# Edge counts from a column of ones in the gather table, with four changes of order in a graph block on one Trainium2 core

## The chip, the cores and the metric

The kernel runs on one core of one Trainium2 chip. TensorE (PE) multiplies matrices, VectorE (DVE), ScalarE (ACT) and GpSimd (POOL) work on tiles of 128 partitions, and SyncE (SP) issues DMAs. ACT and POOL issue DMAs too. The metric is the device time of one execution in microseconds (us): the median over timed runs.

## The reference, cut to what matters

6250 nodes have rows of 256 numbers, and 100,000 edges lead from `src` to `dst`; `dst` is sorted and skewed, so the first nodes have many more edges than the last.

```python
xn = layernorm(x)
# (1) mean over the incoming edges
Wh  = xn @ W + b
h   = segment_sum(Wh[src], dst) / maximum(segment_sum(ones, dst), 1)
# (2) linear attention over all nodes, 8 heads, feature map elu + 1
x1  = x + h + attention(xn) @ wo + bo
# (3) top-1 mixture of 8 experts, at most 977 rows each
logits = layernorm(x1) @ gate_w + gate_b;  e = argmax(softmax(logits))
y   = (relu(layernorm(x1) @ w1[e] + b1[e]) @ w2[e] + b2[e]) * prob[e]
out = x1 + y
```

## The kernel before, in words

The nodes are 49 tiles of 128 rows. One program per engine is written by hand; semaphores (`S["..."]`, counted up, waited for with `wait_ge`) are all that orders the engines.

**Prologue.** Rows are normalised; each is split into a high fp16 part and a scaled low fp16 part (`tall`, 512 fp16 columns, low part times 2048) and stored in DRAM as `table`. Then the keys of all tiles are projected and summed (`project`, `sum_keys` on PE; `keys`, `features` on DVE and ACT), and the matrix `ms` of the attention is formed. While this goes on, POOL already gathers for tile 0 and PE adds one group of edges in 25 of these key steps (`TICKS`, `sum_some`).

**Gather.** POOL gathers the table rows of 128 edges with one indirect DMA (L566); four such are a group, and `gathered` is a ring of `RQ = 7` groups. There are 196 groups, 784 gathers. A group whose edges fall in two tiles is summed for both, so PE and DVE handle 244 (group, tile) pairs. For each pair DVE builds four one-hot matrices (L1291, ring `onehot` of `OQ = 4`), and PE adds `onehot^T @ gathered` to the PSUM bank `pA` (L875). Before the change, PE also adds `ones^T @ onehot` to the bank `pD` (L878): its diagonals hold the number of edges of each node. `slots` tells POOL that a ring place is free, `oh_slots` the same of a one-hot buffer to DVE.

**Steps.** After `ms`, all engines run `step(t)` for t = 0 to 50. In step t, DVE does in this order: `late` (remaining one-hots), `degrees(t)` (count, L1359 to L1365), `next_tile` (up to four one-hots of tile t+1), `combine(t)`, `node_out(t-1)`, `place(t-2)`, `plan`, `shares(t)`, `queries(t+1)`, `residual(t)` (L1380, L1382), `route(t-1)`, `post` of a job. PE does `project_sum(t-1)` (L940 to L944), `count`, `query` (L921), `divisor` (L929), `expert` (L966), `hidden` (L975), the transposes `turn_sums` (L984) and `turn_rows` (L992), then the edge sum of tile t+1. ACT does `ready` (L680), `query` (L692), `divisor`, `job_rows`, `deviation`, `hidden` (relu, L730), `softmax` (L708), `columns` (L722, copies the transposes and signals `t_sb`, for which PE's next `project_sum` waits). POOL scatters the rows of a tile to their expert (L519) when it is five groups past the end of the tile two later, and writes out a finished job (`finish`, L506); both stand in its queue between gathers.

**Jobs.** A job is 128 rows of one expert. From step `T0 = 10` on each step runs the middle part of one job: `plan(t - T0 + LEAD)` three steps ahead picks the first expert that has 128 unserved rows among the tiles placed so far, and a dummy job (rows of a pad tile, nothing written) if none has. What is left after step 50 (`END`), partly filled tiles included, runs in a tail loop of `expert`, `hidden`, `turn_rows` on PE and `post` and `plan` on DVE.

**Weights.** ACT issues eight DMAs of 1 MB (L673) for all output weights `w2s` right after `ms` and before its `query(0)`. SP loads the first-layer weights `w1b` of each job in two halves (L402).

The wait that ends a job's relu is one semaphore for all eight pieces:

```python
for h, (name, ph) in enumerate((("h0_ps", pH0), ("h1_ps", pH1))):   # ACT hidden, L727
    a.wait_ge(S[name], j + 1)
    for c in range(FC // 2): ins = a.activation(...)                  # L730
ins.then_inc(S["h_sb"], 1)                                            # L732
```

## Time and profile before

| what | value |
|---|---|
| median of 3 timed runs | 1618.29 us (1617.28 to 1618.33) |
| span of the profiled execution | 1943.8 us |
| PE, weight load, DVE, ACT, POOL busy | 65%, 43%, 49%, 26%, 47% |
| granted TensorE clock, mean | 0.823 |
| first gather starts | 92.08 us |
| `ready(0)`, `ready(23)`, `ready(48)` on ACT (L680) | 333.36, 1182.07, 1783.04 us |
| last job's write (L506) | 1934.87 us |

The span runs from the first to the last instruction of the profiled execution; the page shows no other time of that execution, and it lies 325.5 us above the median of the timed ones. Times of rows are us from the start of the span. A step is best read from one L680 to the next, since there is one per tile.

### The profile page before, as it was taken

What the parts mean: (1) busy time and instruction counts of PE and PEld (TensorE: products, weight loads), DVE (VectorE), ACT (ScalarE), POOL (GpSimd) and SP (SyncE); (2) the same over time, 40 slices, a digit from 0 to 9 for tenths busy, and PEclk for the clock granted to TensorE, in tenths of its full rate; (3) what the DMA queues carried; (4) which work ended last, traced back from release to release, by engine and by line L of the source; (5) the groups of instructions that cost most, each with busy time, mean ns of one, the idle gap of its engine ahead of it and who ended that gap; (6) DMA issues with size and microseconds to landing.
All of it is one profiled execution on the core that took longest, in us unless ns stands there. A gap on an engine that the chain in (4) does not pass through costs nothing.

```text
span 1943.8 us, 34137 instructions
## 1 busy us (share of the span) xinstructions
PE 1260.6 (65%) x5864; PEld 828.4 (43%) x5865; DVE 957.9 (49%) x3464; ACT 510.3 (26%) x1337; POOL 917.5 (47%) x963
## 2 busy tenths in 40 slices
PE   3666673355454464767656676786786887887785
PEld 2354442011122122544434454454564565565675
DVE  7732321123233253555444564565666665677544
ACT  4521111011111111322222232233333333344232
POOL 4465663674567556446544534544444445421111
PEclk9998985676677576788777887898998888888899
DMA  7562227332223233434333433433443434433342
GB/s 225 157 200 77 85 83 225 90 96 72 77 84 100 85 89 114 131 96 139 104 122 95 129 99 113 132 123 105 137 137 114 143 124 129 126 100 99 119 150 85
DMA packets 141731, 228.88 MB, mean 118 GB/s; under 512 B 29856, under 2 KB 86723, under 8 KB 141618
## 3 DMA queue, kind: packets, MB, share of 16 engines
q0 software_dynamic: 42800, 115.65, 19.7%
q1 hardware_dynamic: 89134, 103.26, 17.3%
q10 hardware_dynamic: 9684, 8.93, 1.5%
q14 instruction: 98, 0.80, 0.1%
q8 instruction: 15, 0.25, 0.0%
HBM read 194.65 MB, written 34.81 MB: 118 GB/s over the span
## 4 chain that ended last, share of the span: by engine, by line
issue 30%; PE 28%; DVE 20%; DVEq 10%; another core or an unknown queue 6%; ACT 3%; ACTq 1%; POOL 1%; DMA 1%; SPq 0%; POOLq 0%
PE pA L875 6%; PE pY L966 6%; PE pH L975 5%; DVE shared L1349 3%; PE pH L854 2%; DVEq L1299 2%; DVEq L1304 1%; DVE onehot L1291 1%; PE pX L944 1%; PE pD L878 1%; DVEq L269 1%; ACTq L673 1%; DVEq L1291 1%; POOL shared L566 1%
## 5 line engine op out<-in xcount | busy, mean ns | idle before, releaser
L566 POOL DMA_INDIRECT shared<-table,idx x784 | 770.0, 982 | 419.8 <-issue 262.9
L875 PE MATMUL pA<-shared,onehot 128*128 x976 | 323.4, 427 | 281.7 <-issue 237.5
L875 PEld LDWEIGHTS pA<-shared,onehot 128*128 x976 | 97.7, 100 | 514.8 <-issue 450.6
L1291 DVE TENSOR_TENSOR onehot<-tile_iota,dst_t 128x512 f32 x244 | 163.6, 693 | 274.8 <-issue 139.0
L519 POOL DMA_INDIRECT rows<-rows_sb,row_at x49 | 49.9, 1018 | 422.8 <-issue 422.8
L975 PE MATMUL pH<-shared 128*128 128x128 f32 x1664 | 212.6, 285 | 36.9 <-issue 36.8
L966 PE MATMUL pY<-w2s,shared 128*128 x832 | 204.5, 399 | 43.7 <-issue 26.1
L975 PEld LDWEIGHTS pH<-shared 128*128 128x128 f32 x1664 | 207.4, 201 | 44.2 <-issue 41.6
L966 PEld LDWEIGHTS pY<-w2s,shared 128*128 128x128 f32 x832 | 160.8, 200 | 74.2 <-issue 53.3
L680 ACT ACTIVATE shared<-pA,rdeg 128x256 f32<-128x256 f32 x49 | 23.2, 473 | 531.3 <-issue 406.9
L1359 DVE CUSTOM_DVE_ANT_1 pD<-pD,ident 128x512 f32<-128x512 f32 x49 | 34.3, 700 | 249.3 <-issue 129.0
L692 ACT ACTIVATE shared<-pQ,bqs 128x128 f32<-128x128 f32 x196 | 55.8, 368 | 383.6 <-remote 252.7
L730 ACT ACTIVATE shared<-pH,b1s 128x128 f32<-128x128 f32 x416 | 116.2, 373 | 137.5 <-PE pH L975 105.8
L940 PE MATMUL pX<-wgs,shared 128*128 128x264 f32 x98 | 50.6, 612 | 115.2 <-issue 103.7
L506 POOL DMA_INDIRECT out_dram<-shared,jtok x52 | 51.6, 992 | 137.9 <-issue 137.9
L878 PE MATMUL pD<-onehot,c 128*128 x244 | 102.8, 421 | 9.1 <-issue 8.0
L854 PE MATMUL pH<-shared,w2s 128*128 128x257 f32 (+1 forms) x196 | 60.2, 436 | 59.6 <-DVE w2s L1276 44.6
L1349 DVE RECIPROCAL shared<-shared 128x256 f32<-128x256 f32 x49 | 85.9, 1753 | 21.7 <-ACT shared L698 13.7
L921 PE MATMUL pQ<-xts,wqs 128*128 (+1 forms) x392 | 67.6, 324 | 21.5 <-issue 21.5
L944 PE MATMUL pX<-shared 128*128 128x264 f32 x196 | 78.2, 542 | 0.0
L940 PEld LDWEIGHTS pX<-wgs,shared 128*128 128x128 f32 x98 | 20.5, 262 | 130.0 <-issue 129.7
L854 PEld LDWEIGHTS pH<-shared,w2s 128*128 128x128 f32 (+1 forms) x196 | 39.6, 213 | 76.0 <-DVE w2s L1276 51.3
(270 smaller groups left out, 1828.4 us busy)
## 6 DMA issues: line engine op xcount, KB each, us to landing
shared<-in_L_ffn_w_dram SPq DMA_DIRECT2D x104, 512.0 KB
shared<-table,idx POOLq DMA_INDIRECT x784
w2s<-in_L_ffn_w_dram ACTq DMA_DIRECT2D x8, 1024.0 KB
rows<-rows_sb SPq DMA_DIRECT2D x7, 1040.0 KB
shared<-rows SPq DMA_DIRECT2D x52, 130.0 KB
shared<-in_L_ffn_b_dram SPq DMA_DIRECT2D x52, 128.0 KB
shared<-in_x_dram SPq DMA_DIRECT2D x12, 512.0 KB, 9.5
table<-w2s SPq DMA_DIRECT2D x12, 512.0 KB, 3.0
```

The source lines that it names most:

```text
L566: g.indirect_dma_start(gathered[:, s * G + j, :], None, table[:, :], bass.IndirectOffsetOnAxis(ap=idx[:, q * G + j:q * G + j + 1], axis=0) ...
L730: ins = a.activation(hs[:, h * FC // 2 + c, :], ph[:, c * P:(c + 1) * P], ACT.Relu, bias=b1s[:, bass.ds(e * FC + h * FC // 2 + c, 1)])
L854: ins = pe.matmul(gp[k][:, 0:DX], kr[0:rows_n, b, k * P:(k + 1) * P], xall[0:rows_n, t, :], start=False, stop=last)
L875: m = pe.matmul(pA[:, :], onehot[:, n % OQ, j, :], gathered[:, (f % RQ) * G + j, :], start=False, stop=stop)
L878: m = pe.matmul(pD[:, :], ones16, onehot[:, n % OQ, :, :].rearrange("p g n -> p (g n)"), start=False, stop=False)
L921: ins = pe.matmul(pQ[:, m * P:(m + 1) * P], wqs[:, k, m * P:(m + 1) * P], xts[:, bass.ds(t, 1), k, :].rearrange("p t n -> p (t n)"), start ...
L940: pe.matmul(pX[:, 0:GW], st[:, 0:P], wgs[:, 0, :], start=True, stop=False)
L944: ins = pe.matmul(pX[:, 0:GW], qn[:, m * P:(m + 1) * P], ms[:, m, :], start=False, stop=(m == DK - 1))
L966: ins = pe.matmul(pY[:, 0:D], hs[:, c, :], w2s[:, bass.ds(e * FC * D + c * D, D)], start=(c == 0), stop=(c == FC - 1))
L975: ins = pe.matmul((pH0, pH1)[h][:, c * P:(c + 1) * P], w1b[:, h, k, c * P:(c + 1) * P], xjt[:, k * P:(k + 1) * P], start=(k == 0), stop=(k ...
L1291: v.tensor_tensor(onehot[:, n % OQ, :, :], tile_iota[:, :].rearrange("p (a n) -> p a n", a=1).broadcast_to([P, G, P]), dst_t[:, bass.ds(ch ...
L1349: k(v.reciprocal(qn, qn))
```

## The change

1. The table's column 255 of the high part is set to 1 and that of the low part to 0. A normalised row adds up to 0, so the last column is the negative sum of the others: the last row of `gnn_w` is subtracted from the other 255 (`last_row`, DVE) and its place is taken by `gnn_b`. Column 255 of `pA` is then the edge count; `pD`'s counting matmuls, its 128x512 reduction on DVE and `mask` go, and so does the small matmul that added `bo` in `project_sum`; `bo` is added in `residual`.
2. PE counts `oh_slots` up at the first matmul of a pair instead of after the last, and the counter starts at 3 instead of 4; DVE makes its first one-hot in the key steps one tick later.
3. ACT runs `columns(t)` before `softmax(t-1)`.
4. ACT signals `h_sb` after each half of the relu; PE waits for a half before the first and before the fifth pair of `expert`'s matmuls.
5. `T0` is 8 instead of 10.
6. SP issues one 1 MB load of `w2s` in each of the steps 0 to 7; ACT issues none.

```diff
-T0 = 10
+T0 = 8
@@ SP
+            def load_out(e):
+                sp.dma_start(w2s[:, bass.ds(e * FC * D, FC * D)].rearrange("p (c d) -> p c d", c=FC),
+                             w2[bass.ds(e, 1), :, :].rearrange("e (c p) d -> p (e c) d", p=P)).then_inc(S["w_big"], 16)
...
+                if big:
+                    load_out(t)
                 if not isinstance(t, int) or 1 <= t <= NT:
                     stored(t - 1)
@@ ACT
-                a.activation(tall[:, t, 0:D], xall[:, t, 0:D], ACT.Copy).then_inc(S["ln_hi"], 1)
+                a.activation(tall[:, t, 0:DC], xall[:, t, 0:DC], ACT.Copy).then_inc(S["ln_hi"], 1)
...
-            for e in range(NX):
-                a.dma_start(w2s[:, e * FC * D:(e + 1) * FC * D].rearrange("p (c d) -> p c d", c=FC),
-                            w2[e, :, :].rearrange("(c p) d -> p c d", p=P)).then_inc(S["w_big"], 16)
...
-                ins.then_inc(S["h_sb"], 1)
+                    ins.then_inc(S["h_sb"], 1)
...
+                columns(t, inner or t < NT, turn)
                 if inner or 1 <= t <= NT:
                     softmax(t - 1)
-                columns(t, inner or t < NT, turn)
@@ PE
-            pe.sem_inc(S["oh_slots"], OQ)
+            pe.sem_inc(S["oh_slots"], OQ - 1)
...
-                    m = pe.matmul(pD[:, :], ones16, onehot[:, n % OQ, :, :].rearrange("p g n -> p (g n)"), start=False, stop=False)
-                    m.then_inc(S["oh_slots"], 1)
-                    if final:
-                        pe.matmul(pD[:, 0:1], zero16, any16[:, 0:1], start=False, stop=True).then_inc(S["agg_done"], 1)
+                        if j == 0:
+                            m.then_inc(S["oh_slots"], 1)
+                        if j == G - 1:
+                            m.then_inc(S["agg_done" if final else "slots"], 1)
...
-                    pe.matmul(pD[:, :], zero16, any16, start=True, stop=False)
...
-                    pe.matmul(pX[:, 0:D], two16[:, :], bo16[:, :], start=False, stop=False)
...
-                    pe.wait_ge(S["h_sb"], j + 1)
-                    pe.sem_inc(S["pe_hold"], 1)
...
                     for c in range(FC):
+                        if c % (FC // 2) == 0:
+                            pe.wait_ge(S["h_sb"], j * 2 + (1 if c == 0 else 2))
+                            pe.sem_inc(S["pe_hold"], 1)
@@ DVE
+            def last_row():
+                v.wait_ge(S["w_in"], 16 * 7)
+                c.mark(v.tensor_tensor(wgs[:, 0, 0:D], wgs[:, 0, 0:D], w_last, ALU.subtract))
+                c(v.tensor_tensor(wgs[0:P - 1, 1, 0:D], wgs[0:P - 1, 1, 0:D], w_last[0:P - 1, :], ALU.subtract))
+                v.sem_inc(S["wg_ok"], 1)
...
-                    k(v.tensor_tensor_reduce(out=counts, in0=counts, in1=ident[:, :].rearrange("p (a n) -> p a n", a=1).broadcast_to([P, G, P]),
-                                             scale=1.0, scalar=0.0, op0=ALU.mult, op1=ALU.add, accum_out=cnt[:, 0:1]))
-                    k.mark(v.tensor_scalar(mask[:, :], cnt[:, 0:1], 1.0, None, ALU.min))
-                    k.mark(v.tensor_scalar(deg[:, 0:1], cnt[:, 0:1], 1.0, None, ALU.max))
-                    k(v.tensor_scalar(deg[:, 1:2], cnt[:, 0:1], 1.0, LO, ALU.max, ALU.mult))
+                    k.mark(v.tensor_scalar(deg[:, 0:1], pA[:, DC:D], 1.0, None, ALU.max))
+                    k(v.tensor_scalar(deg[:, 1:2], pA[:, DC:D], 1.0, LO, ALU.max, ALU.mult))
...
-                    k.mark(v.scalar_tensor_tensor(tg[:, :], gcon[:, 2, :], mask[:, 0:1], xgs[:, t, :], ALU.mult, ALU.add))
...
-                    v.scalar_tensor_tensor(tb, bgb, mask[:, 0:1], xres, ALU.mult, ALU.add).then_inc(S["tb_ok"], 1)
+                    v.tensor_tensor(tb, bob, xres, ALU.add).then_inc(S["tb_ok"], 1)
...
-                        if t - 2 in TICKS:
+                        if t - 2 in TICKS[1:]:
```

On DVE, at the head of each inner step, the count stands between the last one-hots of the tile and the load of the next tile's bounds. Before:

```order
L1356 REGISTER_ALU
L1359 ISA pD,cnt<-pD,ident 128x512 [waits agg_done]
L1359 ISA cnt 128x1
L258 ISA
L1361 TENSOR_SCALAR mask<-cnt 128x1 [waits agg_c]
L1362 TENSOR_SCALAR deg<-cnt 128x1
L1363 TENSOR_SCALAR deg<-cnt 128x1
L258 REGISTER_ALU
L1365 RECIPROCAL rdeg<-deg 128x2 [waits agg_c]
```

After (line numbers of the changed kernel):

```order
L1353 REGISTER_ALU
L1355 TENSOR_SCALAR deg<-pA 128x1 [waits agg_done]
L1356 TENSOR_SCALAR deg<-pA 128x1
L254 ISA
L1358 RECIPROCAL rdeg<-deg 128x2 [waits agg_c]
```

The wide reduction, the read of its accumulator, the mask and one wait are gone; both `deg` read PSUM directly.

On ACT, between the last copy of `ms` (L670, afterwards L674) and the first query. Before:

```order
L670 ACTIVATE shared<-pQ 128x264 [waits m_ps]
L670 ACTIVATE shared<-pT 128x264
L673 DMA w2s<-in_L_ffn_w_dram 128x8x256 x8
L692 ACTIVATE shared<-pQ,bqs 128x128 [waits qd_ps]
L692 ACTIVATE shared<-pQ,bqs 128x128 x3
```

After:

```order
L674 ACTIVATE shared<-pQ 128x264 [waits m_ps]
L674 ACTIVATE shared<-pT 128x264
L692 ACTIVATE shared<-pQ,bqs 128x128 [waits qd_ps]
L692 ACTIVATE shared<-pQ,bqs 128x128 x3
L680 ACTIVATE shared<-pA,rdeg 128x256 [waits rdeg_ok]
```

The eight DMAs have left ACT's queue; they stand in SP's, one behind each step's load of the residual rows.

On PE, at the head of the tail loop, the end of the loop's preparation and `expert`. Before:

```order
L297 REGISTER_ALU
L297 TENSOR_LOAD planw
L297 ISA x2
L960 REGISTER_ALU
L966 ISA [waits h_sb,y_sb]
L966 MATMUL pY<-w2s,shared 128x256
```

After:

```order
L293 REGISTER_ALU
L293 TENSOR_LOAD planw
L293 ISA x2
L962 ISA [waits y_sb]
L964 ISA [waits h_sb]
L964 MATMUL pY<-w2s,shared 128x256
```

The wait for `h_sb` stands where it stood, but is met by half of the relu; a second one has come four pieces later.

## Rows read from the trace of the kernel before

**Rows 1.** Busy time of each stretch, five engines, then granted clock, DMA share, GB/s

```profile
310.00:337.00 27.00, 3.21 (x15) 2.66 (x13) 4.06 (x12) 3.12 (x10) 3.86 (x5) 0.55 1.05 335
363.00:394.00 31.00, 9.45 (x23) 2.37 (x23) 0.69 (x1) 0.00 (x0) 19.64 (x22) 0.54 0.30 86
1509.70:1532.30 22.60, 17.69 (x92) 12.37 (x91) 15.27 (x58) 8.36 (x22) 9.23 (x12) 0.85 0.42 132
1845.00:1926.00 81.00, 67.08 (x449) 61.40 (x448) 41.14 (x161) 26.12 (x87) 8.60 (x10) 1.00 0.47 146
```

**Rows 2.** Timeline (start, duration, instruction, idle before): ACT's `ready`, tiles 23, 36, 37, 48

```profile
1182.07 0.47 ACT L680 ACTIVATE shared<-pA,rdeg 128x256 f32<-128x256 f32 x1 [18.05 <-issue]
...
1509.66 0.47 ACT L680 ACTIVATE shared<-pA,rdeg 128x256 f32<-128x256 f32 x1 [6.24 <-issue]
1532.28 0.47 ACT L680 ACTIVATE shared<-pA,rdeg 128x256 f32<-128x256 f32 x1 [6.24 <-issue]
...
1783.04 0.47 ACT L680 ACTIVATE shared<-pA,rdeg 128x256 f32<-128x256 f32 x1 [5.90 <-DVE rdeg L1365]
```

**Rows 3.** Timeline of POOL: gathers

```profile
229.67 0.95 POOL L566 DMA_INDIRECT shared<-table,idx  x1 [0.30 <-issue]
...
343.04 0.94 POOL L566 DMA_INDIRECT shared<-table,idx  x1 [27.96 <-PE pA L875]
```

**Rows 4.** Timeline of POOL: a scatter alone, and a scatter with a job's write

```profile
641.66 1.02 POOL L519 DMA_INDIRECT rows<-rows_sb,row_at  x1 [5.13 <-issue]
644.36 0.97 POOL L566 DMA_INDIRECT shared<-table,idx  x1 [1.68 <-issue]
...
903.54 1.02 POOL L519 DMA_INDIRECT rows<-rows_sb,row_at  x1 [4.33 <-issue]
...
908.39 1.00 POOL L566 DMA_INDIRECT shared<-table,idx  x1 [1.80 <-PE pA L875]
```

**Rows 5.** Longest wait of DVE, 1486 to 1623 us: in total, times, longest

```profile
DVE tile_iota L1331 <- issue: 8.0, 7, 2.2
```

**Rows 6.** Timeline of the tail: PE and ACT

```profile
1869.57 0.38 PE L992 MATMUL pT<-ident,shared 128*128 128x128 f32 x2
1869.87 1.14 ACT L730 ACTIVATE shared<-pH,b1s 128x128 f32<-128x128 f32 x4 [0.64 <-PE pH L975]
...
1871.47 3.72 PE L966 MATMUL pY<-w2s,shared 128*128 x16 [1.52 <-ACT shared L730]
```

**Rows 7.** Timeline of ACT at the end of the prologue

```profile
307.04 22.64 ACTq L673 DMA_DIRECT2D w2s<-in_L_ffn_w_dram  x7
329.72 1.14 ACT L692 ACTIVATE shared<-pQ,bqs 128x128 f32<-128x128 f32 x4 [22.46 <-issue]
```

**Rows 8.** Timeline of DVE in the step of Rows 2

```profile
1523.15 0.23 DVE L1380 SCALAR_TENSOR_TENSOR tg<-gcon,mask,xgs 128x8 f32<-128x8 f32 x1
...
1530.88 0.70 DVE L1359 CUSTOM_DVE_ANT_1 pD<-pD,ident 128x512 f32<-128x512 f32 x1 [1.09 <-issue]
...
1531.74 0.14 DVE L1362 TENSOR_SCALAR deg<-cnt 128x1 f32<-128x1 f32 x1
```

**Rows 9.** Timeline of PE, steps 49 and 50

```profile
1794.41 1.22 PE L940 MATMUL pX<-wgs,shared 128*128 128x264 f32 x2 [3.32 <-ACT shared L722]
1811.61 5.28 PE L966 MATMUL pY<-w2s,shared 128*128 x16 [0.81 <-issue]
```

**Rows 10.** The page's costliest groups: line, engine, op, count, busy, mean ns, idle before

```profile
L878 PE MATMUL pD<-onehot,c 128*128 x244 | 102.8, 421 | 9.1 <-issue 8.0
```

**Rows 11.** Timeline of the key steps: PE and DVE

```profile
250.04 1.13 PE L875 MATMUL pA<-shared,onehot 128*128 x4
251.72 0.69 DVE L1291 TENSOR_TENSOR onehot<-tile_iota,dst_t 128x512 f32 x1 [2.71 <-PE pD L878]
...
260.09 1.04 PE L875 MATMUL pA<-shared,onehot 128*128 x4
```

**Rows 12.** The page's costliest groups: a job's write

```profile
L506 POOL DMA_INDIRECT out_dram<-shared,jtok x52 | 51.6, 992 | 137.9 <-issue 137.9
```

More of the change, by code:

```diff
@@ L16 @@
 DX = D + 1
+DC = D - 1
 HEADS = 8
@@ L205, in gps_block @@
         deg = sb("deg", [P, 2])
-        mask = sb("mask", [P, 1])
-        cnt = sb("cnt", [P, 1])
-        tg = sb("tg", [P, NX])
         rdeg = sb("rdeg", [P, 2])
@@ L410, in load_bias, with step @@
                 sp.dma_start(b2r, b2[bass.ds(e, 1), :].broadcast_to([P, D])).then_inc(S["b2_in"], 16)
-            def step(t, rows=True, weights=True, bias=True):
+            def load_out(e):
+                sp.dma_start(w2s[:, bass.ds(e * FC * D, FC * D)].rearrange("p (c d) -> p c d", c=FC),
+                             w2[bass.ds(e, 1), :, :].rearrange("e (c p) d -> p (e c) d", p=P)).then_inc(S["w_big"], 16)
+            def step(t, rows=True, weights=True, bias=True, big=False):
                 if not isinstance(t, int) or 1 <= t <= NT:
@@ L423, in step @@
                     load_bias(t - T0, bias == "first")
+                if big:
+                    load_out(t)
                 if not isinstance(t, int) or 1 <= t <= NT:
                     stored(t - 1)
-            step(0, False, False, False)
+            step(0, False, False, False, True)
             with sp.Fori(1, T0 - 2) as t:
-                step(t, False, False, False)
-            step(T0 - 2, "first", False, False)
-            step(T0 - 1, True, "first", False)
+                step(t, False, False, False, True)
+            step(T0 - 2, "first", False, False, True)
+            step(T0 - 1, True, "first", False, True)
             step(T0, True, True, "first")
@@ L605, in _ @@
             with nc.allow_non_contiguous_dma(reason="bias columns"):
[L606 to L611 removed]
+                a.dma_start(gbias[:, :], bo.rearrange("(k p) -> p k", p=P)).then_inc(S["w_in"], 16)
+            a.wait_ge(S["consts"], 9)
             def std_(i):
@@ L812, in _ @@
                                           start=(i == 0), stop=(i == DK - 1))
-                    for w in range(3):
+                    for w in range(2):
                         for k in range(DK):
@@ L873, in add @@
                     for j in range(G):
-                        stop = final and j == G - 1
-                        m = pe.matmul(pA[:, :], onehot[:, n % OQ, j, :], gathered[:, (f % RQ) * G + j, :], start=False, stop=stop)
-                        if j == G - 1 and not final:
-                            m.then_inc(S["slots"], 1)
-                    m = pe.matmul(pD[:, :], ones16, onehot[:, n % OQ, :, :].rearrange("p g n -> p (g n)"), start=False, stop=False)
-                    m.then_inc(S["oh_slots"], 1)
-                    if final:
-                        pe.matmul(pD[:, 0:1], zero16, any16[:, 0:1], start=False, stop=True).then_inc(S["agg_done"], 1)
+                        m = pe.matmul(pA[:, :], onehot[:, n % OQ, j, :], gathered[:, (f % RQ) * G + j, :], start=False,
+                                      stop=final and j == G - 1)
+                        if j == 0:
+                            m.then_inc(S["oh_slots"], 1)
+                        if j == G - 1:
+                            m.then_inc(S["agg_done" if final else "slots"], 1)
                     pe.reg_add(pair_r, pair_r, 1)
@@ L1144, in rest @@
                 v.wait_ge(S["ln_hi"], t + 1)
-                v.tensor_tensor(dif[:, t % NB, :], xall[:, t, 0:D], tall[:, t, 0:D], ALU.subtract).then_inc(S["ln_dif"], 1)
+                v.tensor_tensor(dif[:, t % NB, 0:DC], xall[:, t, 0:DC], tall[:, t, 0:DC], ALU.subtract).then_inc(S["ln_dif"], 1)
             def gate_columns():
                 c.mark(v.memset(new_row[:, :], 0.0))
-                v.wait_ge(S["w_in"], 16 * 7)
                 c.mark(v.memset(wide_b[:, 0, :, :], 1.0))
-                c.mark(v.memset(two16[0:1, :], 1.0))
-                c.mark(v.memset(two16[32:33, :], 1.0 / LO))
-                for w in range(2):
-                    for k in range(DK):
-                        c.mark(v.tensor_copy(wide_b[:, 1 + w, k, :], gbias[:, w, k:k + 1].broadcast_to([P, P])))
+                for k in range(DK):
+                    c.mark(v.tensor_copy(wide_b[:, 1, k, :], gbias[:, k:k + 1].broadcast_to([P, P])))
                 c.wait()
                 v.sem_inc(S["gc_in"], 1)
-                c.mark(v.tensor_copy(bo16[0:1, :], bo_f[0:1, :]))
-                c(v.tensor_copy(bo16[32:33, :], bo_f[32:33, :]))
-                c(v.tensor_tensor(bo_f[32:33, :], bo_f[32:33, :], bo16[32:33, :], ALU.subtract))
-                c(v.tensor_scalar(bo16[32:33, :], bo_f[32:33, :], LO, None, ALU.mult))
+            def last_row():
[3 more added lines that the diff above has]
+                v.sem_inc(S["wg_ok"], 1)
             def gate_sums():
@@ L1373, in residual @@
                 def residual(t):
-                    k = part("tb_c", t)
-                    v.wait_ge(S["rdeg_ok"], t + 1)
-                    hold(v, "dve_hold")
                     v.wait_ge(S["xr_in"], t * 16 + 16)
                     hold(v, "dve_hold")
-                    k.mark(v.scalar_tensor_tensor(tg[:, :], gcon[:, 2, :], mask[:, 0:1], xgs[:, t, :], ALU.mult, ALU.add))
-                    assert k.n == K["tb_c"]
-                    v.scalar_tensor_tensor(tb, bgb, mask[:, 0:1], xres, ALU.mult, ALU.add).then_inc(S["tb_ok"], 1)
+                    v.tensor_tensor(tb, bob, xres, ALU.add).then_inc(S["tb_ok"], 1)
                 def node_out(t):
@@ L1387, in node_out @@
                     v.wait_ge(S["tb_ok"], t + 1)
-                    hold(v, "dve_hold")
-                    v.wait_ge(S["tb_c"], t + 1)
                     hold(v, "dve_hold")
```

49 lines of the change are left out of this document (23 added, 26 removed).

## The prediction

> **What bounds the kernel now.** I read the busy time of stretches first, then the timeline of the engine that does not rest in each, then who waited for whom. The profiled execution spans 1943.8 us and the page shows nothing of it outside the span; the median of the timed runs is 1618.29 us, 325.5 us less. The stretches show where such a difference can sit: from 363 to 394 us PE runs 23 matmuls in 31 us, DVE 1 instruction and ACT none, while POOL goes on at its usual pace [rows 1]. Such creeping stretches come back through the whole prologue and the first half. Over the last 25 steps a step takes 24.04 us on average ((1783.04 - 1182.07) / 25), against 22.6 us where nothing creeps (1532.28 - 1509.66) [rows 2], so they hold only 25 x 1.4 = 36 us there. I take them as belonging to the profiled execution, read each term from rows free of them, and subtract the terms from the median as they stand.
>
> Without them three regimes remain. (a) While tiles have many edges POOL sets the pace: a gather every 0.95 + 0.30 = 1.25 us [rows 3], 5.0 us a group of four. A scatter takes 2.7 us up to the next gather, 4.85 us when a finished job goes with it [rows 4], and my estimate is 1 us of sequencer time in front, part of the idle 4 to 5 us there. (b) Later a step takes 22.6 us [rows 2] although POOL would need less: DVE's instructions stand without a gap that another engine causes. Its waits over six steps are all "issue", its own sequencer, the longest 2.2 us [rows 5]; none is for PE. PE, ACT and POOL have room. (c) In the tail PE does one job after another and waits for ACT's relu each time [rows 6].
>
> Where (a) gives way to (b): POOL's step of n new groups costs 5.0 n + about 5.5 us (4.85 + 1 less the 0.30 already in a gather), which is 22.6 at n = 3.4. The number of edges up to a node grows as the root of its number, so tiles 0 to 15 hold 112 of the 196 groups, tile 16 has 3.4, and the 33 tiles from 16 on have (196 - 112) / 33 = 2.5 on average. So about 32 steps (17 to 48) belong to DVE.
>
> **The change part by part.**
>
> *Output weights by SP.* ACT is held 22.64 us by seven of its eight DMAs and starts query(0) at 329.72 [rows 7]. PE and DVE stand almost still meanwhile [rows 1], and POOL, whose ring is full, idles 27.96 us until 343.04 [rows 3]. After the change ACT goes straight to query(0). POOL loses its idle time as far as PE comes back before the ring is full: between 0 and 28 us; I take 22, the length of ACT's hold. The same 8 MB now go out in eight steps. In the stretch 310 to 337 the DMA engines are full at 335 GB/s [rows 1], so each MB fills them for 3.1 us, beside gathers that POOL must see landed one group later. Cost between 0 and 8 x 3.1 = 25; I take 3, since a POOL period of 5 us hides most of such a delay. Behind SP's load stand only the next steps' row transfers, which have over 20 us. PE wants all eight before step 9, and the last is issued in step 7.
> The Trainium skill, page "Trainium Kernel Development and Optimization", section "Key Constraints", holds against this part that DMAs of SP, ACT and POOL "all run on the same 16 DMA engines and interleave", and that several issuers save only the sequencer's issue time. By that rule the 24 us of transfer are only moved, and the sum of this part would be near 0. The trace supports the first half (engines full at 335 GB/s) and shows why I differ on the sum: in the burst everybody waits, and later the engines are busy 30 to 42% [rows 1].
>
> *DVE per step.* The reduction starts at 1530.88 and the first `deg` at 1531.74 [rows 8]: 0.86 us go, mask included. In `residual`, `tg` of 0.23 us goes [rows 8]; overlapped with its neighbour it is worth some 0.2. Together 1.06 us in each of 32 steps: 34 us. Bounds: 25 steps x 0.86 = 21 and 37 x 1.3 (by the full lengths 0.86 + 0.23 and 0.2 for two waits less) = 48. DVE stays last: after the change PE has 3.3 us less wait for `t_sb` (its wait in steps 49 and 50 is 3.32) [rows 9] and over 2 us less work, ACT's copies are ready earlier, and POOL needs 5.0 n + 5.5 = 18 us at n = 2.5 against 21.5. Near n = 3.2 POOL takes over, two steps later than now; that costs 1 us.
>
> *PE's counting matmuls, `bo` matmul, columns before softmax.* 244 matmuls of 0.42 us [rows 10], overlapped by half, so about 0.2 each or 1 us a step, and three small ones a tile, 0.6 together: some 1.6 us a step of PE. I cost them at nothing inside the steps: POOL's gathers or DVE's chain end later. If that cover failed they would be worth 48 x 1.6 = 77 us.
>
> *Key steps.* DVE's one-hot waits for the counting matmul and starts at 251.72, 1.68 us after the pair's first matmul at 250.04 [rows 11]; released by that first one (a quarter of 1.13 us, and 0.3 to get through) it comes 1.1 us earlier in each of 25 ticks, 27 us at most. I take 0: two ticks take 260.09 - 250.04 = 10.05 us [rows 11], POOL's two groups. The gain would only fill POOL's ring, whose idle time is counted already. The one-hot counter that starts at 3 costs nothing, for DVE's later one-hot is used three groups on.
>
> *Prologue on DVE.* Four copies and two memsets less, two subtractions more: -1 us.
>
> *Relu in halves.* In the tail PE is ready after L992 (1869.57 + 0.38 = 1869.95) and starts L966 at 1871.47, 1.52 us later, on the second half of the relu, which starts at 1869.87; the first half is over by then [rows 6]. Afterwards PE starts at once, and four pieces take 1.86 us, so the second half is ready. 11 jobs x 1.52 = 16.7 us. A job takes 9.0 us now (449 matmuls in 81 us, 50 a job) and 7.5 then; DVE is busy 41.14 us of 81, 4.6 a job, and DMA 47% [rows 1], so both still fit. In steps 49 and 50 the wait of 3.32 us [rows 9] shrinks by the exponential and its table, about 1.6 each: 3.2. Together 20; bounds 8 (loads late) and 24 (`expert` takes 5.28 us there instead of 3.72, partly at the clock's lower level [rows 6, 9]).
>
> *Jobs from step 8.* I put the reference's expert choices into the planner's rule. With T0 = 10 it makes 44 plans, 3 of them dummies, leaves 8, and gives 52 jobs, as the page shows [rows 12]. With T0 = 8 it makes 46 plans; the two new ones are dummies too, for at step 5 and soon after no expert has 128 unserved rows. 8 are left again: 54 jobs, and the tail has 12 as before. The gain is 0; the cost is two more finishes on POOL while POOL sets the pace, 2 x (4.85 - 2.70) = 4 us [rows 4].
>
> Sum: -22 + 3 - 34 + 1 - 1 - 20 + 4 = -69 us. On the median: 1618 - 69 = 1549 us.
>
> **The rivals.**
>
> *POOL holds longer.* The scatter waits 4 to 5 us before it starts even in the first half [rows 4]. If these are real, POOL with its waits covers half of the 32 steps (-17 instead of -34) and the burst's idle returns in part (-10 instead of -22): 1549 + 29 = 1578. For it: POOL never reaches full use in any stretch. Against it: those waits follow creeping stretches.
>
> *PE's chain decides.* If the first steps are bound by PE and DVE and not by POOL, the 1.6 us of PE count in 16 more steps, the key steps give 10 to 27, and DVE's 0.86 counts there too: 16 x 2.5 + 15 = 55 more, 1494. Against it: 5.0 us a group is POOL's own pace.
>
> *Early jobs shorten the tail.* If the two jobs are real, the tail has two fewer at 7.5 us: 1549 - 15 = 1534. Against it: the planner's rule gives the page's 52 exactly.
>
> *The clock falls.* PE has fewer matmuls, and its clock stands at 0.85 in a DVE-bound step and 0.54 in a creeping one [rows 1]. If it stayed at the lower level (1.2 GHz) in the DVE-bound steps, PE's 17.69 us less 2 would become 15.7 x 0.85 / 0.5 = 26.7 us, more than 21.5, and PE would set a step of 26.7: 32 x 4.1 = 131 us lost against 22.6, the other terms (-22 + 3 - 1 - 20 + 4 = -36) kept: 1713 us. It decides once PE's busy time per step exceeds 22.6 us. Against it: the removed work shortens the step as well, so PE's share falls only from 78% to about 73%, and its one long wait per step goes.
> The Trainium skill, page "TensorE: Matmul & The Clock Gate", section "Part 1: The HAM clock gate", says that the clock follows how busy PE has recently been. By that rule this rival is possible; the trace agrees with the direction (0.54, 0.85 and 1.00 at PE shares of 30%, 78% and 83%) [rows 1].
>
> **How the numbers follow.** The forecast 0.60 (its own range 1530 to 1570), POOL holds longer 0.19, PE's chain 0.12, the tail 0.04, the clock 0.03, and 0.02 that gains and costs cancel to within 0.2%, which is about what a measurement here can tell from no change. Faster 0.95, same 0.02, slower 0.03. The range takes in the bounds of the hidden idle and of DVE's steps and most of the two larger rivals: 1505 to 1595.
>
> **What would show it.** ACT's L692 follows its copies of `ms` within 3 us, and POOL's idle before the first step's gather is under 10 us. A quiet step of three pairs takes 21.5 us and DVE waits in it only on "issue". L966 in the tail follows L992 without the wait for L730 and the period is 7.5 us. 54 writes by L506. The forecast is wrong if late steps stay at 22.6, if POOL or PE waits appear on DVE there, if the tail keeps 9.0 us, or if the clock of late steps is near 0.5.

## The result and the profile after

| kernel | median | ratio to before, 95% interval |
|---|---|---|
| before | 1617.78 us (1616.0 to 1618.33) | 1 |
| after | 1552.9 us (1551.53 to 1557.38) | 0.9606 (0.9594 to 0.9617) |

The change takes 64.9 us off; the forecast was 69. The number came out well, but three terms of its sum did not (output weights, column of ones, T0), and their errors nearly cancel.

The profiled execution of the changed kernel spans 1549.8 us and took 1551.53: it has no creeping stretches. The rows below are set against those of before. The first fence is the busy time of stretches (PE, weight load, DVE, ACT, POOL, each with its number of instructions, then granted clock, DMA share, GB/s): two late steps and 81 us of the tail.

```profile
1151.00:1171.55 20.55, 16.96 (x93) 11.39 (x92) 14.90 (x55) 8.27 (x21) 13.19 (x14) 0.92 0.53 163
1171.55:1191.37 19.82, 16.41 (x96) 12.23 (x95) 14.16 (x54) 8.27 (x22) 9.92 (x11) 1.00 0.44 143
1440.00:1521.00 81.00, 77.38 (x513) 71.92 (x512) 47.99 (x196) 30.52 (x100) 10.81 (x11) 0.96 0.57 172
```

In the tail PE is busy 96% of the stretch, where it was 83% [rows 1], and runs 513 matmuls in it, not 449. The clock of the late steps is at or near its upper level (2.4 GHz), so the rival of the falling clock did not come true.

The timeline of ACT and of PE behind the copies of `ms` answers to [rows 7]:

```profile
248.96 0.39 ACT L674 ACTIVATE shared<-pT 128x264 f32<-128x264 f32 x1
256.64 1.14 ACT L692 ACTIVATE shared<-pQ,bqs 128x128 f32<-128x128 f32 x4 [7.29 <-PE pQ L919]
```

```profile
247.56 1.08 PE L1056 MATMUL pT<-w2s,shared 128*128 128x264 f32 x2
253.00 1.89 PE L875 MATMUL pA<-shared,onehot 128*128 x4 [4.37 <-POOLq L550]
254.68 1.92 PE L919 MATMUL pQ<-xts,wqs 128*128 128x128 f32 x8
```

ACT's hold is gone, but L692 follows after 7.7 us (256.64 - 248.96) and not within the 3 I gave as a sign. PE first adds a pair of edges, and waits 4.37 us for POOL to report a landed group. That is the first hint that POOL, and not ACT, sets the time here. The other half of the sign holds: POOL's longest idle time from 246 to 330 us is 1.79 us.

The timeline of DVE at the head of a late step, then at the end of the tail that of PE and ACT, which answer to [rows 8] and [rows 6]:

```profile
1150.45 0.16 DVE L1355 TENSOR_SCALAR deg<-pA 128x1 f32<-128x1 f32 x1 [1.05 <-issue]
1150.71 0.17 DVE L1358 RECIPROCAL rdeg<-deg 128x2 f32<-128x2 f32 x1
1151.83 0.24 DVE L1328 TENSOR_SCALAR tile_iota<-tile_iota 128x128 f32<-128x128 f32 x1 [0.96 <-issue]
```

```profile
1465.04 0.38 PE L990 MATMUL pT<-ident,shared 128*128 128x128 f32 x2
1465.25 3.62 PE L964 MATMUL pY<-w2s,shared 128*128 x16
...
1472.50 3.62 PE L964 MATMUL pY<-w2s,shared 128*128 x16
```

```profile
1463.55 1.14 ACT L730 ACTIVATE shared<-pH,b1s 128x128 f32<-128x128 f32 x4 [3.65 <-PE pH L973]
1465.33 1.14 ACT L730 ACTIVATE shared<-pH,b1s 128x128 f32<-128x128 f32 x4 [0.64 <-PE pH L973]
```

DVE waits at the head of the step on its own sequencer only ("issue"), as forecast; the step of 21.5 us that I gave as a sign takes 20.55 and 19.82 (the first fence), for a reason given at the column of ones. `expert` (L964) starts before the second half of the relu does, with no wait, and this job takes 7.25 us (1472.50 - 1465.25; eight in a row take 7.3 on average) where one took 9.0. The page counts L510 54 times, as the planner's rule gave.

### The profile page after: what moved, and what is told of

Same layout as the page of the kernel before. It is cut to its first block, busy times and chain, and to the rows that moved or that the text cites. A ratio compares the mean times of both kernels' runs of the same rounds, so it can differ in the third digit from the quotient of the medians.

```text
span 1549.8 us, 33330 instructions
## 1 busy us (share of the span) xinstructions
PE 1124.6 (73%) x5569; PEld 762.9 (49%) x5570; DVE 906.8 (59%) x3297; ACT 513.5 (33%) x1355; POOL 918.1 (59%) x966
## 3 DMA queue, kind: packets, MB, share of 16 engines
q0 software_dynamic: 42896, 115.65, 25.1%
## 4 chain that ended last, share of the span: by engine, by line
DVE 29%; issue 27%; POOL 16%; PE 11%; DVEq 9%; ACT 2%; DMA 2%; POOLq 2%; SPq 1%; ACTq 0%
POOL shared L570 16%; DVE shared L1346 4%; PE pY L964 3%; PE pH L973 2%; PE pA L875 2%; DVEq L1301 2%; DVEq L1296 2%; PE pH L855 2%; DVE shared L1466 1%; DVE shared L1464 1%; DMA shared<-table,idx 1%; DVE shared L1455 1%; DVE shared L1469 1%; DVE stats L1387 1%; DVE shared L1463 1%
## 5 line engine op out<-in xcount | busy, mean ns | idle before, releaser
L875 PE MATMUL pA<-shared,onehot 128*128 x976 | 341.5, 470 | 263.2 <-POOLq L550 165.3
L964 PE MATMUL pY<-w2s,shared 128*128 x864 | 203.6, 390 | 5.8 <-issue 4.6
L973 PEld LDWEIGHTS pH<-shared 128*128 128x128 f32 x1728 | 201.4, 192 | 2.7
L973 PE MATMUL pH<-shared 128*128 128x128 f32 x1728 | 201.7, 275 | 0.0
L680 ACT ACTIVATE shared<-pA,rdeg 128x256 f32<-128x256 f32 x49 | 23.2, 473 | 473.3 <-DVE rdeg L1358 473.3
L964 PEld LDWEIGHTS pY<-w2s,shared 128*128 128x128 f32 x864 | 164.0, 195 | 30.0 <-issue 7.3
L510 POOL DMA_INDIRECT out_dram<-shared,jtok x54 | 54.9, 1016 | 112.7 <-issue 112.7
L1355 DVE TENSOR_SCALAR deg<-pA 128x1 f32<-128x1 f32 x49 | 7.8, 158 | 184.6 <-PE pA L875 153.5
L692 ACT ACTIVATE shared<-pQ,bqs 128x128 f32<-128x128 f32 x196 | 55.7, 370 | 73.1 <-PE pQ L927 65.8
L708 ACT ACTIVATE lg<-lg,sc 128x8 f32<-128x8 f32 x49 | 14.7, 301 | 143.5 <-DVE sc L1403 143.3
L941 PE MATMUL pX<-shared 128*128 128x264 f32 x196 | 61.8, 446 | 0.0
L855 PE MATMUL pH<-shared,w2s 128*128 128x257 f32 (+1 forms) x196 | 53.9, 398 | 9.5 <-DVE w2s L1273 9.2
L919 PE MATMUL pQ<-xts,wqs 128*128 (+1 forms) x392 | 58.4, 294 | 1.7
L938 PE MATMUL pX<-wgs,shared 128*128 128x264 f32 x98 | 43.0, 528 | 20.7 <-issue 16.5
```

The costliest lines, as they stand in the source:

```text
L708: a.activation(lg[:, 1, :], lg[:, 0, :], ACT.Exp, bias=sc[:, 4:5], accum_out=sc[:, 5:6]).then_inc(S["ex_ok"], 1)
L855: ins = pe.matmul(gp[k][:, 0:DX], kr[0:rows_n, b, k * P:(k + 1) * P], xall[0:rows_n, t, :], start=False, stop=last)
L875: m = pe.matmul(pA[:, :], onehot[:, n % OQ, j, :], gathered[:, (f % RQ) * G + j, :], start=False, stop=final and j == G - 1)
L919: ins = pe.matmul(pQ[:, m * P:(m + 1) * P], wqs[:, k, m * P:(m + 1) * P], xts[:, bass.ds(t, 1), k, :].rearrange("p t n -> p (t n)"), start ...
L941: ins = pe.matmul(pX[:, 0:GW], qn[:, m * P:(m + 1) * P], ms[:, m, :], start=False, stop=(m == DK - 1))
L964: ins = pe.matmul(pY[:, 0:D], hs[:, c, :], w2s[:, bass.ds(e * FC * D + c * D, D)], start=(c == 0), stop=(c == FC - 1))
```

## The experiments

None of the twelve leaves out a part of the computation. In each one's trace the span lies within 4 us of the median, so they show the steps without the creeping that the trace of before has. The end of a step is read from ACT's `ready` (L680, up to four lines lower in some of these kernels), in us from the start:

| kernel | ready(0) | ready(1) | ready(9) | ready(16) | ready(48) | span |
|---|---|---|---|---|---|---|
| before + SP's loads | 263.24 | 318.14 | 596.11 | 770.81 | 1460.05 | 1620.5 |
| before + relu halves | 284.92 | 327.02 | 591.80 | 767.15 | 1457.88 | 1599.5 |
| before + column of ones | 278.70 | 322.99 | 586.11 | 751.04 | 1403.24 | 1561.4 |
| after | 260.04 | 315.91 | 592.60 | 760.73 | 1411.29 | 1549.8 |
| after, T0 = 10 | 257.80 | 314.80 | 583.74 | 750.47 | 1402.18 | 1540.1 |
| the same, loads by ACT | 276.56 | 321.16 | 582.43 | 748.60 | 1399.90 | 1538.3 |
| the same, burst by SP | 262.56 | 320.29 | 581.76 | 747.91 | 1398.74 | 1537.3 |
| T0 = 13, loads by ACT | 277.60 | 322.13 | 582.76 | 740.59 | 1392.16 | 1526.0 |
| after + counting on PE | 259.07 | 314.54 | 592.26 | 762.67 | 1414.76 | 1549.5 |
| after + reduction on DVE | 259.48 | 315.69 | 594.60 | 766.67 | 1442.34 | 1578.1 |

The second row stands in for before. Up to ready(9) no job has run and the two kernels do the same; from there to ready(48) it is an assumption, that PE does not wait for the relu in the steps.

### Output weights: who issues them, and when

```diff
 # kernel before, ACT
-            for e in range(NX):
-                a.dma_start(w2s[...], w2[e, ...]).then_inc(S["w_big"], 16)
 # SP, in the steps 0 to 7
+                if big:
+                    load_out(t)
```

> The kernel before with one part of the change: SP issues a 1 MB load of the output weights in each of the steps 0 to 7, ACT issues none. My term was -22 + 3: about 1599 us, 0.988 of the kernel before, and in its trace POOL's idle time in front of the first step's gather falls from 27.96 to under 10 us. Rival 1 (the transfer of 8 MB is only moved, the engines that move it are shared anyway): 1618 us, 1.00, with the lost time back as later waits of PE for landed gathers. Rival 2 (nothing of the idle time returns and the loads collide with nothing): -28, 0.983.

Measured: 1622.99 us against 1616.68, ratio 1.0043 (1.003 to 1.0057): 5 to 9 us slower. Where it goes is in the table. ready(0) comes 21.7 us earlier, the size of my 22; at ready(1) only 8.9 are left, at ready(9) it is 4.3 us behind. The next two fences are POOL's timeline with the loads by ACT (the kernel with relu halves): the two longest idle times of the burst, and a scatter in step 5 with its next gather.

```profile
266.80 0.94 POOL L566 DMA_INDIRECT shared<-table,idx  x1 [2.72 <-DMA shared<-table,idx]
...
294.59 0.94 POOL L566 DMA_INDIRECT shared<-table,idx  x1 [6.74 <-PE pA L875]
...
470.44 1.01 POOL L519 DMA_INDIRECT rows<-rows_sb,row_at  x1 [0.30 <-issue]
471.75 0.97 POOL L566 DMA_INDIRECT shared<-table,idx  x1 [0.30 <-issue]
```

The same scatter in the kernel with SP's loads, SP's load before it, and a scatter three steps later:

```profile
458.07 0.40 SPq L414 DMA_DIRECT2D w2s<-in_L_ffn_w_dram  x1
```

```profile
466.88 1.01 POOL L526 DMA_INDIRECT rows<-rows_sb,row_at  x1 [2.01 <-issue]
469.81 0.97 POOL L573 DMA_INDIRECT shared<-table,idx  x1 [1.92 <-issue]
...
572.84 1.01 POOL L526 DMA_INDIRECT rows<-rows_sb,row_at  x1 [0.30 <-issue]
574.26 0.97 POOL L573 DMA_INDIRECT shared<-table,idx  x1 [0.41 <-issue]
```

Two things differ from what I assumed. POOL idles 6.74 us in the burst's end, not 27.96 [rows 3]: PE and DVE are held 22 us while POOL goes on with little loss, and POOL is what counts in step 1. And a load costs POOL waits around the next scatter, here (2.01 - 0.30) + (1.92 - 0.30) = 3.3 us: step 5 takes 36.0 us instead of 32.7. That is as long as the transfer at the full rate (my estimate from [rows 1], 3.1 us a MB), but it is the dearest of the loads. The scatters behind the loads of the steps 2 to 7 lose 1.7, 2.6, 3.3, 2.8, 2.9 and 0.1 us; together that is 13.4, the 13.2 that the kernel falls back from ready(1) to ready(9). The last scatter, at 572.84 above, loses 0.1; its load was issued at 561.35, 11.5 us before it, and those of the others 6.6 to 8.9 us before. With the loads by ACT the same scatters wait 0.30 us on either side, one of them 0.45. The loads of the steps 0 and 1 have no scatter close behind them (the first scatter starts at 384.74), and POOL's gathers stand 0.30 to 0.39 us apart from 253 us until then. So what a load costs shows at the scatter, and goes with where it comes before it. What the scatter waits for the profile does not show ("issue"), and no run moved a load to another place in its step.

```diff
 # after with T0 = 10
-T0 = 8
+T0 = 10
-            step(T0 - 2, "first", False, False, True)
-            step(T0 - 1, True, "first", False, True)
+            step(T0 - 2, "first", False, False)
+            step(T0 - 1, True, "first", False)
 # then, loads by ACT
-                if big:
-                    load_out(t)
+            for e in range(NX):              # ACT, behind ms
+                a.dma_start(w2s[...], w2[e, ...]).then_inc(S["w_big"], 16)
```

> The changed kernel with T0 = 10 and the output weights issued by ACT behind ms again. Theory now (from the first four runs: in a trace without creeping stretches POOL idles only some 9 us in ACT's burst, and each 1 MB load beside the gathers makes POOL's step 2 to 3 us longer, so moving the loads to SP costs about what it gives or more): 3 to 6 us under the kernel with T0 = 10 and SP's loads, 1535 to 1538 us, 0.950 of the kernel before. Rival (my original term of -22 + 3 holds once the other parts are in): 19 us more, 1560 us, 0.965.

Measured: 1538.95 us, 0.9513 (0.95 to 0.9526), against 1541.11, 0.9534 (0.9521 to 0.9547), with SP's eight single loads and the same T0. Some 2 to 3 us for ACT's burst; the two intervals still touch, so what is excluded is the 19 us of my term, not 0. The table has the same shape: ready(0) 18.8 us later, ready(48) 2.3 earlier. Beside the other parts the single loads cost less: from ready(1) to ready(9) the kernel with them loses 7.7 us (268.94 against 261.27), 1.1 a load, where it was 1.9 alone. Again it is at the scatters: the five with a load 8.7 to 10.6 us before them lose 0.7 to 2.9 us each, in no order of that distance, and the sixth, with 13.1 us, nothing. The load of step 1, with no scatter behind it, costs 0.8 us here at a gather 7.4 us later (331.94 - 324.55); together 7.7.

```diff
 # the same eight loads on SP, behind ms
             sp.dma_start(xres, x_t[0, :, :]).then_inc(S["xr_in"], 16)
+            for e in range(NX):
+                sp.dma_start(w2s[...], w2[e, ...]).then_inc(S["w_big"], 16)
```

> The changed kernel with T0 = 10; the eight 1 MB loads are issued by SP, all at once behind ms. This parts ACT's hold from the transfer. If ACT's hold of 22 us is what costs time there: better than ACT's burst by up to 9 us (POOL's idle time), 1528 us, 0.945, with ready(0) near 258 us. If the full DMA engines are what costs (gathers land late whoever issues): the same as ACT's burst within 3 us.

Measured: 1536.66 us, 0.9494 (0.9481 to 0.9507). ready(0) comes 14 us before that of ACT's burst, ready(1) 0.9 us before, and the time is 2.3 us less, inside the intervals. ACT's hold of 22 us is worth next to nothing. Sent as a burst the 8 MB delay POOL by some 4 us in this kernel (its idle times between 260 and 285 us, less 0.30 each, where the changed kernel has none), about as much as ACT's burst does (5 us) and less than the 7.7 of the single loads.

### Jobs from step 8

The edit is the first of the two diffs in front of the kernel with T0 = 10 and the loads by ACT.

> The changed kernel with T0 = 10 again (52 jobs, 3 of them dummies, 12 jobs in the tail as before). My term for T0 = 8 was +4, for two dummy jobs more in steps where POOL sets the pace: 4 us less than the changed kernel, 1549 us, 0.958 of the kernel before. Rival 1 (the two early jobs shorten something after all): 15 us more than the changed kernel, 1568 us, 0.969. Rival 2 (a dummy's work lies beside other work on every engine): the same as the changed kernel within 0.1%, 0.9605.

Measured: 1541.11 us, 0.9534 (0.9521 to 0.9547): 11.8 us less than the changed kernel. T0 = 8 costs 12 us, three times my term. The difference arises from ready(5) to ready(12): 0.9 us (474.72 against 473.84) becomes 10.5 (671.59 against 661.11). POOL's timeline with T0 = 8 around step 8, two scatters and the gathers behind them:

```profile
566.45 1.02 POOL L523 DMA_INDIRECT rows<-rows_sb,row_at  x1 [0.68 <-issue]
569.23 1.27 POOL L570 DMA_INDIRECT shared<-table,idx  x1 [1.76 <-issue]
...
590.87 1.02 POOL L523 DMA_INDIRECT rows<-rows_sb,row_at  x1 [1.42 <-issue]
593.64 1.02 POOL L570 DMA_INDIRECT shared<-table,idx  x1 [1.75 <-issue]
```

and with T0 = 10:

```profile
561.85 1.02 POOL L523 DMA_INDIRECT rows<-rows_sb,row_at  x1 [0.30 <-issue]
563.17 1.27 POOL L570 DMA_INDIRECT shared<-table,idx  x1 [0.31 <-issue]
...
583.94 1.02 POOL L523 DMA_INDIRECT rows<-rows_sb,row_at  x1 [0.30 <-issue]
585.27 0.97 POOL L570 DMA_INDIRECT shared<-table,idx  x1 [0.31 <-issue]
```

No job is written out yet in these rows; what a job brings at first is its 1 MB of first-layer weights, SP's L398, here 9.4 us before the second scatter:

```profile
581.47 1.07 SPq L398 DMA_DIRECT2D shared<-in_L_ffn_w_dram  x2
```

That scatter loses (1.42 - 0.30) + (1.75 - 0.31) = 2.6 us, the same pattern as with a load of `w2s`. A write later takes 1.6 us of POOL where no load comes close before it (698.98 to 700.59), not the 2.15 of the disturbed [rows 4]; together some 4 us a job of the 5.9 measured. I had priced the write alone. That it is the weights, and not the job's rows or biases (0.13 MB each), is argued from the pattern; no run left one of them out.

```diff
-T0 = 10
+T0 = 13
```

> The changed kernel with T0 = 13 and the output weights by ACT: 49 jobs, no dummy, 8 left after the loop and 12 in the tail as before; the three jobs less are those of steps 10, 11 and 12. Theory now (a job in a step where POOL sets the pace costs 4 to 6 us, from the 11.8 us of T0 = 8 against 10): 6 to 12 us under the kernel with T0 = 10 and ACT's loads, about 1527 us, 0.944. Rival 1 (my term of 2.15 us a job on POOL, 6 us in all, partly covered): 3 to 6 us. Rival 2 (step 10 to 12 are already DVE's, where a dummy's post hides nothing and its rows pay later): 0.

Measured: 1529.72 us, 0.9465 (0.9452 to 0.9478), 9.2 us less than with T0 = 10 and the same loads. ready(16) is 8.0 us earlier and ready(48) 7.7; the tail has its 12 jobs as before (133.8 us behind ready(48) here, 138.4 there, and 137.5 in the next kernel, which has the same work: single executions differ by as much). Three jobs less at 5.9 us would be 18. In the traces the gain is 10.5 us at ready(13) and falls back to 8.0 at ready(16); why part of it is lost there was not tested. The page counts 49 writes, as the planner's rule gives.

```diff
 # T0 = 13, and the eight loads as SP's burst
```

> The changed kernel with T0 = 13 and the eight 1 MB loads issued by SP at once behind ms: the two changes that helped, together. If they add up: 2 us under the kernel with T0 = 13 and ACT's burst, 1527 us, 0.9445. If the burst's issuer makes no difference: 1530 us, 0.9465.

Measured: 1530.41 us, 0.945 (0.9437 to 0.9464). Not told apart from ACT's burst. These two are the fastest kernels of the study, 23 us under the changed one.

### The column of ones

```diff
 # after, with the other five parts undone (T0 = 10, w2s by ACT, h_sb once a job,
# softmax before columns, one-hot given back late; only the last is shown)
-                        if j == 0:
-                            m.then_inc(S["oh_slots"], 1)
+                    pe.matmul(pD[:, 0:1], zero16, any16[:, 0:1], start=True, stop=True).then_inc(S["oh_slots"], 1)
```

> The kernel before with one part of the change: the edge count comes from the column of ones (no counting matmul on PE, no 128x512 reduction, no mask on DVE, bo added in the residual); the one-hot buffer is given back after the last matmul of a pair (by a matmul of one column), softmax before columns, relu whole, T0 = 10, output weights by ACT. My term was -34 + 1 - 1: 1584 us, 0.979, and a late step of three pairs takes 21.5 us in its trace against 22.6. Rival 1 (PE's chain or its 1.6 us a step counts in the earlier steps too): -34 - 40 to -55, 1530 to 1545 us, 0.945 to 0.955. Rival 2 (in the changed kernel's trace a late step takes 20.2 us, 2.4 less than before, so the reduction costs DVE more than its own 0.86 us): 32 x 2.4 = -77, 1541 us, 0.952, with the 1.2 us of idle time in front of the one-hots' tile_iota gone as well.

Measured: 1559.75 us, 0.9641 (0.9628 to 0.9654): -57 us, between my term (-34) and the rivals (-74 and more). By the table, against the kernel with relu halves: 6.2 us before ready(0), of which 5.7 are left at ready(9), 10.4 from ready(9) to ready(16), 38.5 in the 32 late steps (1.20 each), and the rest, 2.3, behind ready(48).

```diff
 # after + reduction on DVE
+                    k(v.tensor_tensor_reduce(out=counts, in0=counts, in1=ident..., accum_out=cnt[:, 0:1]))
                     k.mark(v.tensor_scalar(deg[:, 0:1], pA[:, DC:D], 1.0, None, ALU.max))
```

> The changed kernel with the 128x512 reduction and the read of its accumulator put back on DVE, ahead of deg (it reads a bank that nobody else uses and its sum isn't used; PE stays as it is). My term was 0.86 us in each of the steps from 17 on: 28 us, 1581 us, 0.978. Theory now (a late step got shorter by 1.2 us, of which tg and a wait 0.2 to 0.3, and steps 10 to 16 are DVE's too, where 10 us went): 30 + 9 = 39 us, 1592 us, 0.985. Rival (only steps with DVE last and without POOL's pace): under 25 us.

Measured: 1580.59 us, 0.9769 (0.9756 to 0.9783): 27.7 us more than the changed kernel. That is my 28, but the places differ a little: 25.1 us in the 32 late steps, 0.78 each, 3.9 from ready(9) to ready(16) and 2.0 before, with 2.7 less behind ready(48). DVE's timeline there shows the 0.80 us from the reduction to `deg`, and the idle time ahead of `tile_iota`:

```profile
1170.74 0.70 DVE L1358 CUSTOM_DVE_ANT_1 pD<-pD,ident 128x512 f32<-128x512 f32 x1 [1.10 <-issue]
1171.54 0.16 DVE L1360 TENSOR_SCALAR deg<-pA 128x1 f32<-128x1 f32 x1
...
1172.94 0.23 DVE L1330 TENSOR_SCALAR tile_iota<-tile_iota 128x128 f32<-128x128 f32 x1 [0.98 <-issue]
```

The trace of before has 2.17 us ahead of `tile_iota`, which made me think that the reduction lengthens that gap too. It does not. The gap is 0.96 to 0.98 us in the three traces shown, with the reduction or without:

```profile
1181.08 0.70 DVE L1360 CUSTOM_DVE_ANT_1 pD<-pD,ident 128x512 f32<-128x512 f32 x1 [1.09 <-issue]
...
1183.32 0.23 DVE L1332 TENSOR_SCALAR tile_iota<-tile_iota 128x128 f32<-128x128 f32 x1 [0.97 <-issue]
```

(the kernel with relu halves, which has before's steps). The step of [rows 2], from ready(36) to ready(37), lasts 21.04 us in it (1225.17 - 1204.13) and 19.82 in the changed kernel (1191.37 - 1171.55); the 22.6 of the trace of before still held 1.6 us of its own, 1.2 of them in that gap. That is why the changed step lies under my 21.5.

```diff
 # after + counting on PE
+                        if j == G - 1:
+                            pe.matmul(pD[:, :], ones16, onehot[:, n % OQ, :, :]..., start=True, stop=True)
                         m = pe.matmul(pA[:, :], onehot[:, n % OQ, j, :], gathered...)
```

> The changed kernel (T0 = 8, loads by SP) with the 244 counting matmuls (128x512 into the unused bank pD, ahead of a pair's last edge matmul) put back on PE, and no one waiting for them. My term for PE's share of the column of ones was 0, covered by POOL's gathers or DVE's chain: the same as the changed kernel within 0.3%, 0.961 to 0.963. Rival (PE's time counts wherever PE ends a step): up to 244 x 0.2 to 0.4 = 50 to 100 us. Between them: where an early step ends with PE's last pair after POOL's last gather, each step's last counting matmul counts, 17 x 0.3 = 5 us.

Measured: 1553.29 us, 0.961 (0.9595 to 0.9625), the same as the changed kernel. The page's line of the edge matmuls shows a part of the cover: PE's idle time for landed groups shrinks by 10 us. First with the counting matmuls, then without:

```profile
L877 PE MATMUL pA<-shared,onehot 128*128 x976 | 354.0, 440 | 251.5 <-POOLq L550 155.0
```

```profile
L875 PE MATMUL pA<-shared,onehot 128*128 x976 | 341.5, 470 | 263.2 <-POOLq L550 165.3
```

### The relu in halves

```diff
-                ins.then_inc(S["h_sb"], 1)
+                    ins.then_inc(S["h_sb"], 1)
...
+                        if c % (FC // 2) == 0:
+                            pe.wait_ge(S["h_sb"], j * 2 + (1 if c == 0 else 2))
```

> The kernel before with one part of the change: the relu is signalled in halves, and PE waits for a half before the first and the fifth pair. My term was -20: 1598 us, 0.988; the tail's period falls from 9.0 to 7.5 us and the wait of 1.52 us before each expert goes. Rival 1 (the loads of a job's weights or rows come too late for 7.5 us a job, so the wait moves there): -8 or less, 0.995, with a period near 8.3 us. Rival 2 (the halves also shorten the steps before the tail, where PE works close to its limit): more than -25, under 0.985.

Measured: 1601.3 us, 0.9902 (0.9886 to 0.9917): -15.4 us. In the traces the stretch behind ready(48) falls from 160.5 (1620.5 - 1460.05) to 141.6 us (1599.5 - 1457.88), 18.8 less, and with the column in both kernels from 158.2 to 138.5, 19.7 less. The 3 to 4 us between trace and timing are in no place that I could name.

### Two orders

```diff
 # one-hot given back late; the counter starts at 4, DVE's first one-hot a tick earlier
-                        if j == 0: m.then_inc(S["oh_slots"], 1)
+                    pe.matmul(pD[:, 0:1], zero16, ...).then_inc(S["oh_slots"], 1)
```

> The changed kernel, but a one-hot buffer is given back after the last matmul of its pair (by a matmul of one column), the counter starts at 4 and DVE makes its first one-hot a tick earlier, as before. My term for this part was 0: 1553 us, 0.961, with only the filling of POOL's ring changed. Rival (the key steps' 250 to 275 us are the path, and in the trace with the early release ms is copied 5 to 7 us sooner): 5 to 9 us more, 1559 us, 0.965, with ready(0) later by as much and the difference still there in ready(48).

Measured: 1550.76 us, 0.9583 (0.957 to 0.9596): 2 us less, if anything, though ready(0) is the same (260.07) and ready(48) 2.0 us later in the trace. The early release brings no gain that can be measured; the rival is out. `ms` is copied 1.7 us sooner with it (248.96 against 250.70), and nothing comes of that by ready(0).

```diff
 # ACT
+                if inner or 1 <= t <= NT:
+                    softmax(t - 1)
                 columns(t, inner or t < NT, turn)
-                if inner or 1 <= t <= NT:
-                    softmax(t - 1)
```

> The changed kernel, but ACT runs softmax(t-1) before columns(t), as before. My term was 0 in the steps (PE's wait for t_sb is covered) and some 1.6 x 2 = 3 us in steps 49 and 50: 1553 to 1556 us, 0.961 to 0.9625. Rival (PE's wait for t_sb, 63.5 us over all steps in the kernel with whole columns order before and under 20 in the changed one, counts in the steps where PE's edge sum comes last, 2 to 16): 15 x 0.6 = 9 us more, 0.9665.

Measured: 1553.3 us, 0.9603 (0.9585 to 0.9621), no difference. PE's wait for `t_sb` is covered in the steps, as forecast, and the 3.2 us that I expected in steps 49 and 50 are not there: behind ready(48) it takes 139.0 us (1551.5 - 1412.54) against 138.5.

## Why the prediction was right, and where not

*The regimes were right, their border was not.* POOL sets the first ten steps at its 1.25 us a gather (gathers stand 0.30 us apart in step 5 without load), DVE the late ones, PE and ACT the tail. But DVE's part of the change counts from step 10 on and not from step 17. One reason is in my price of POOL's step, 5.0 n + 5.5: without a load close before it a scatter takes 1.31 us up to the next gather (471.75 - 470.44), not the 2.70 of [rows 4], so POOL's step is shorter and DVE takes over earlier; this is my sum and not a run. From the regimes came the parts that were priced at nothing: PE's counting (measured +0.4), columns before softmax (+0.4), key steps (-2).

*"Read each term from rows free of them": right for durations, wrong for waits.* The step of 22.6 us, POOL's 27.96 us and the gaps around the scatter [rows 2, 3, 4] were not free of the creeping: in the traces without it the same step takes 21.04, POOL waits 6.74, and the scatter's gaps are 0.30.

*Output weights by SP, -22 + 3 = -19: wrong.* Alone it is +6 us (+5 to +9), in the changed kernel some +2. Two steps failed. "POOL loses its idle time ... I take 22, the length of ACT's hold": the hold is real, and ready(0) comes 22 us sooner, but POOL had only some 9 us of idle time to lose (6.74 and 2.72, less 0.30 each). And "a POOL period of 5 us hides most of such a delay": alone the loads cost 13.2 us in seven steps (8.9 us ahead at ready(1) become 4.3 behind at ready(9)), beside the other parts 7.7, against the 3 that I took and my upper bound of 25 (8 x 3.1). The rule that I had set against this part, of the Trainium skill, page "Trainium Kernel Development and Optimization", section "Key Constraints", that the DMAs of all issuers share the same engines and that spreading them over issuers only saves issue time, came closer than I did: by it the part gives about 0, +6 and +2 were measured, and whether ACT or SP issues the burst makes no difference that can be told (2.3 us).

*Column of ones, -34 on DVE and 0 on PE: the late steps right, the early ones missed; -57 measured.* A late step gains 1.20 us against 1.06, and the reduction by itself costs 27.7 us against 28, though some of that outside the late steps. I had let DVE's part begin at step 17: 10 us go in the steps 10 to 16, and 6 before ready(0). My rival on PE's chain named the early steps and the key steps, but its price was 55 us, and in the changed kernel PE's counting costs nothing. What of the 57 beyond DVE's own work (28 for the reduction, some 6 for `tg`) is PE's in the slower kernel was not tested by itself: the counting matmuls were put back only where the one-hot buffers are given back early.

*Relu, 16.7 + 3.2: right in sum.* -15 by the timed runs, -19 to -20 by the traces. The 3.2 for the order of softmax is 0, and a job takes 7.3 us and not 7.5: PE waits for nothing and is 96% busy, and 11 x (9.0 - 7.3) = 19 us. Two errors cancel in this term.

*T0 = 8, +4: the mechanism incomplete.* The jobs are dummies and the tail is as long as before. But a dummy loads its 1 MB of weights like any other job, and that was not in the price: +12.

The single parts add up to +6.3 - 56.9 - 15.4 + 11.8 = -54 us against -65 together. The measured kernels also form a chain in which each step adds parts to the last: column of ones 1616.7 to 1559.8, relu with the two orders to 1539.0, single loads by SP to 1541.1, T0 = 8 to 1552.9. That is -56.9, -20.8, +2.2 and +11.8, where I had -34, -20, -19 and +4. So the relu (with the orders) and the loads come out 5 and 4 us better beside the other parts than alone; why is open. The errors are -23 for the column, +21 for the loads and +8 for T0. That they nearly cancel is luck, and the forecast is only 4 us off because of it.

## What to carry to other kernels

Look first at how far a profiled execution lies from the timed ones. If it is longer, its durations still serve, but an idle time in it may be its own; a variant of the kernel whose trace does not creep shows the true one. Where indirect gathers set the pace, a megabyte moved beside them is not free, whoever issues it: here 0.5 to 1.2 us a MB in a burst, and as a single load from nothing to 3.3 us, mostly at a scatter of POOL that came 6 to 11 us behind it. Ask of each new job or load what it moves and what stands in the gather's queue just then, dummies included, and let jobs begin only when rows for them are there. And an engine held for 22 us costs only what the engine that sets the pace loses by it.

## What was not expected of the hardware

Of fourteen profiled kernels one, before, crept: its span was 325 us over its timed median, with stretches of 23 matmuls in 31 us [rows 1], where the thirteen others lie within 4 us. What made it creep is not known, and the same steps in two variants ran without it.

A 1 MB load on SP's queue, issued 8.8 us before POOL's scatter (466.88 - 458.07), made POOL wait 3.3 us, split over the two waits around that scatter, while the gathers in between stood 0.30 us apart as before. A load issued 11.5 us before a scatter (572.84 - 561.35) cost 0.1 us, and those with no scatter behind them none in this kernel and some 1 us in two others.
